# Merged jobs, a turn for each pair of scores, and a new order of work in a fused transformer layer

## The reference

```python
h = token_table[x] + segm_table[mask] + pos            # (8, 1024, 192)
n = layernorm(h)                                       # 192 channels
q, k, v = split(n @ w_qkv.T)                           # 12 heads of 16
q = layer_norm(q) * 16 ** -0.5; k = layer_norm(k)      # over the 16 of a head
h = h + (softmax(q @ k.T) @ v) @ w_proj.T              # 1024 x 1024 scores a head
xq = round(clip(layernorm(h) / mean(alpha_a1), -8, 7)) # 4-bit values
x1 = clip(gelu((xq @ wq1.T) * alpha_w1 * mean(alpha_a1) + b1), -10, 10)   # 768 wide
hq = round(clip(x1 / mean(alpha_a2), -8, 7))
out = h + (hq @ wq2.T) * alpha_w2 * mean(alpha_a2) + b2
```

## Time and profile before

| | us |
|---|---|
| median of 3 runs (1069.35 to 1070.07) | 1069.4 |
| profiled execution, span from its first to its last instruction | 1067.6 |
| PE busy (92%) | 979.4 |
| ACT busy (82%) | 872.6 |
| DVE busy (76%) | 813.9 |
| POOL busy (39%) | 411.8 |

### The profile page before, as it was taken

One profiled execution on the slowest core, in us unless ns is written; L12 is line 12 of the kernel. 1 busy time (PEld: TensorE's weight loads), 2 busy tenths in 40 slices (PEclk: granted clock), 3 DMA queues, 4 the chain that ended last, 5 costly groups with the idle time before them and its releaser, 6 DMA issues.

```text
span 1067.6 us, 19577 instructions
## 1 busy us (share of the span) xinstructions
PE 979.4 (92%) x7571; PEld 389.1 (36%) x7571; DVE 813.9 (76%) x2325; ACT 872.6 (82%) x950; POOL 411.8 (39%) x345
## 2 busy tenths in 40 slices
PE   5589999999999999999999999999999999989885
PEld 4333433334342433434343343434334343413223
DVE  5878869788686969878696977869697886825347
ACT  1387788897979889797988979798888989798883
POOL 6555513635343353534435363443526412201000
PEclk9899999999999999999999999999999999999997
DMA  7511200303011040202102040110202000000000
GB/s 162 127 16 16 31 1 2 46 1 64 12 25 22 1 75 1 38 8 58 18 2 45 1 73 3 31 16 16 30 1 45 1 16 1 16 1 1 16 1 31
DMA packets 25762, 28.62 MB, mean 27 GB/s; under 512 B 5027, under 2 KB 22182, under 8 KB 25670
## 3 DMA queue, kind: packets, MB, share of 16 engines
q0 software_dynamic: 16896, 11.80, 9.4%
q1 hardware_dynamic: 8624, 15.55, 4.8%
q10 hardware_dynamic: 150, 0.01, 0.0%
HBM read 21.06 MB, written 6.29 MB: 26 GB/s over the span
## 4 chain that ended last, share of the span: by engine, by line
PE 40%; ACT 30%; DVE 24%; issue 3%; POOL 3%; DMA 0%
ACT probs L682 22%; PE ps_o L1247 12%; PE ps_s L1227 8%; PE ps_j L1271 4%; ACT gelu L676 4%; PE ps_j L1279 3%; PE ps_j L1325 3%; POOL stack L592 3%; PE ps_j L1286 2%; PE ps_j L1292 2%; ACT L676 2%; ACT L682 2%; DVE hn L797 2%; PE ps_j L1311 2%; PE ps_j L1296 2%
## 5 line engine op out<-in xcount | busy, mean ns | idle before, releaser
L682 ACT ACTIVATE probs<-ps_s 128x1024 f32<-128x1024 f32 x768 | 736.1, 1023 | 125.5 <-PE ps_s L1227 120.6
L1247 PE MATMUL ps_o<-probs,v_sb 128*32 128x512 f32 x3072 | 394.7, 605 | 0.2 <-DVE o_sb L859 0.2
L1227 PE MATMUL ps_s<-qT,kT 64*128 64x512 f16 x1536 | 264.3, 384 | 35.0 <-ACT probs L682 25.2
L592 POOL TENSOR_TENSOR stack<-sq,stack 128x384 f16<-128x384 f32 x124 | 120.5, 992 | 162.9 <-DVE stack L846 162.9
L1227 PEld LDWEIGHTS ps_s<-qT,kT 64*128 64x128 f16 x1536 | 61.5, 93 | 299.5 <-ACT probs L682 267.6
L525 POOL DMA_INDIRECT h_all<-in_L_tok_token_table,idx x60 | 96.7, 1611 | 59.5 <-DMA h_all<-in_L_tok_segm_table,idx 41.2
L1247 PEld LDWEIGHTS ps_o<-probs,v_sb 128*32 128x32 f32 x3072 | 69.1, 109 | 124.3 <-issue 116.1
L601 POOL TENSOR_TENSOR y_sb<-y_sb,b_row 128x768 f32<-128x768 f32 x14 | 25.4, 1814 | 198.8 <-DVE y_sb L931 198.8
L581 POOL TENSOR_TENSOR sq<-qk 128x384 f32<-128x384 f32 x56 | 46.2, 826 | 139.5 <-DVE qk L894 139.5
L525 POOL DMA_INDIRECT h_all<-in_L_tok_segm_table,idx x56 | 87.2, 1557 | 15.2 <-issue 13.1
L1279 PE MATMUL ps_j<-wh,partsT 128*128 128x384 f16 (+1 forms) x384 | 71.5, 296 | 1.0 <-ACT partsT L663 0.7
(11 more groups left out here) (201 smaller groups left out, 1118.5 us busy)
## 6 DMA issues: line engine op xcount, KB each, us to landing
out<-h_all SPq DMA_DIRECT2D x15, 384.0 KB
h_all<-in_positions SPq DMA_DIRECT2D x7, 768.0 KB
gelu<-in_L_ffn_w SPq DMA_DIRECT2D x2, 576.0 KB
h_all<-in_L_tok_token_table,idx POOLq DMA_INDIRECT x60
h_all<-in_L_tok_segm_table,idx POOLq DMA_INDIRECT x56
probs<-in_L_attn_qkv_weight SPq DMA_DIRECT2D x2, 432.0 KB, 4.7
h_all<-in_positions SPq DMA_DIRECT2D x2, 384.0 KB, 8.0
o_nat<-in_L_ffn_alpha_a SPq DMA_DIRECT2D x1, 384.0 KB
```

Of the source, the lines that this page charges most:

```text
L592: last = nc.gpsimd.tensor_tensor(low, src, high, ALU.subtract)
L682: nc.scalar.activation(probs[:, u % PROBS, 2 * pair:2 * pair + 2], ps_s[:, 2 * pair:2 * pair + 2], ACT.Exp, scale=SCORE_SCALE).then_inc(ex ...
L1227: last = mm(ps_s[:, j], kT[rows, par, head // 2, m * P:(m + 1) * P], qT[rows, par, head // 2, nh * NQ:(nh + 1) * NQ], start=True, stop=True)
L1247: last = mm(ps_o[32 * j:32 * j + 2 * D, :], v_sb[:, par, m, (GH * group + j) * VE:(GH * group + j) * VE + 2 * D], probs[:, u % PROBS, j], ...
```

## The change

1. **Turns.** The plan has a new word s: one pair of scores on PE, one exp on ACT, in the place where it stands. The 48 words of a half-step are spread among heads and jobs; in START_PLAN each line simply begins with s s. The gelus stand at their word g.
2. **Merged jobs**, from half-step 1 on: A, C, G, H and Y take two tiles, I four. Their matmuls write side by side in one bank, and there is one eviction for them. Both norms (N and m) are cut in two, for two tiles each.
3. **A new order** of all words. GpSimd's work has words too: q (square), L (low halves), p (segment gather), t (token gather), a (add the result). W takes banks by its number, as X and B do.
4. n waits for the transposes of D as well as of E before it writes the high halves.

The waits count merged jobs by a function `count`; the rest of the diff replaces `nth` by it.

```diff
 
 
 PLAN = """
-h h o
-Y0 Y1 Y2 F0 Y3 F1
-G0 F2 F3 H0 G1 P0
-h h
-G2 G3 W0 W1 W2 H1 H2 H3
-h l0 h R0
-W3 m0 h
-W4 h
-h N0 W5 I0
-I1 h o A0
-I2 h A1 A2
-h A3 I3
-C0 B0 X0
-X1 B1 r0 X2 X3 B2 X4 X5 r1 B3 h r2 h r3 g h
-h
-h S0 n0
-h n1 o
-D0 x0 E0 C1
-n2 h C2 D1
-E1 n3 h
-D2 h x1
-h D3 E2 x2
-E3 x3 x4 h
-x5 C3 h
+s h o h s
+s F0 q0 F1 F2 s
+s F3 q1 G0 h s
+s G1 P0 H0 s
+s H1 s h W0
+s s h h W1
+s s q2 q3 l0 R0 Y0 W2
+s N0 h s W3
+s h m0 s A0 W4
+s h s h m1 N1 W5
+s s B0 I0
+s s A1 Y1 B1 X0 o p0 X1 r0 B2 r1 X2 x0 X3 g B3 r2 X4 r3 X5 h h
+s S0 L0 n0 s h h
+s s x1 h
+s L1 C0 n1 s o
+s h s h L2
+s s n2 h
+s E0 x2 D0 s h
+s s C1 D1
+s h s h
+s s L3 n3 E1 E2 D2 x3
+s h s
+s h s E3 D3
+s h x4 t0 x5 a0 s
 """
 
 
@@ START_PLAN @@
-h
-h n1.1 D0.1 E0.1 n2.1
...
-w1.2 h D3.2 E3.2
+s s h
+s s h n1.1 D0.1 E0.1 n2.1
...
+s s w1.2 h D3.2 E3.2 q0.2 q1.2 q2.2 q3.2 L0.2 L1.2 L2.2 L3.2
@@ banks @@
-IN_TURN = [w for w in JOBS if w[0] not in "XB"]
+TILES = {"A": 2, "C": 2, "G": 2, "H": 2, "Y": 2, "I": 4}
+IN_TURN = [w for w in JOBS if w[0] not in "XBW"]
+def tiles_of(kind, s0):
+    return TILES.get(kind, 1) if s0 >= 1 else 1
@@ GpSimd, one half-step @@
-                add_result(s0, s)
                 ahead = s0 + GATHER_AHEAD
-                if FIRST_GATHERED <= ahead < HALVES:
-                    add_segments(ahead)
-                    add_tokens(ahead)
-                square(s0, s)
-                split_low(s0, s)
+                for kind, t, at in step_work(s0):
+                    if kind == "a":
+                        add_result(s0, s)
+                    elif kind == "p" and FIRST_GATHERED <= ahead < HALVES:
+                        add_segments(ahead)
+                    elif kind == "t" and FIRST_GATHERED <= ahead < HALVES:
+                        add_tokens(ahead)
+                    elif kind == "q":
+                        square(s0, s, t)
+                    elif kind == "L":
+                        split_low(s0, s, t)
@@ ACT, one half-step @@
-                for u in range(UNITS):
...
+                for kind, t, at in step_work(s0):
+                    if kind == "g" and job_runs("X", s0):
                         for j in range(HB):
                             gelu_out(s0, s, j)
...
+                    elif kind == "s" and attends(s0):
+                        exps(s0, s, t // 2, t % 2)
@@ DVE first_norm (second_norm alike) @@
-                for t in range(TH):
+                here = slice(0, TH) if s0 <= 0 else slice(2 * i, 2 * i + 2)
+                for t in range(TH)[here]:
@@ DVE split_qk @@
+                    dve.wait_ge(job_mm["D"], half * TH + (t - 1))
                     dve.wait_ge(job_mm["E"], half * TH + (t - 1))
@@ DVE, eviction of H and Y @@
-                    tt(h_tile(half, t), ps[:, 0:C], h_tile(half, t), ALU.add).then_inc(job_out["H"], 1)
+                    two = h_all[:, at:at + 2 * C]
+                    tt(two, ps[:, 0:2 * C], two, ALU.add).then_inc(job_out["H"], 1)
...
-                    tt(y_sb[:, t], ps[:, 0:C], s2_row[:], ALU.mult).then_inc(job_out["Y"], 1)
+                    tt(y_sb[:, first:first + 2], ps[:, 0:2 * C].rearrange("p (t c) -> p t c", c=C),
+                       s2_row[:].unsqueeze(1).broadcast_to([P, 2, C]), ALU.mult).then_inc(job_out["Y"], 1)
@@ PE scores @@
-                for j in range(GH):
-                    if j % 2 == 0 and (u or attends(s0 - 1)):
-
-                        pe.wait_ge(exp_done, 2 * UNITS * s + (2 * u - 1 + j // 2))
+                if u or attends(s0 - 1):
+
+                    pe.wait_ge(exp_done, 2 * UNITS * s + (2 * u - 1 + pair))
+                for j in (2 * pair, 2 * pair + 1):
@@ PE job G (A, H, I, Y alike) @@
-                    for k in range(2):
-                        last = nc.tensor.transpose(ps[0:KC, k * P:(k + 1) * P], o_nat[:, t, k * KC:(k + 1) * KC], ident[:])
+                    for n, tile in enumerate(tiles):
+                        for k in range(2):
+                            last = nc.tensor.transpose(ps[0:KC, (2 * n + k) * P:(2 * n + k + 1) * P],
+                                                       o_nat[:, tile, k * KC:(k + 1) * KC], ident[:])
@@ PE, one half-step @@
-                for u in range(UNITS):
-                    if attends(s0):
-                        scores(s0, s, u)
-                    for kind, t, at in unit_work(s0)[u]:
...
+                for kind, t, at in step_work(s0):
+                    if kind == "s" and attends(s0):
+                        scores(s0, s, t // 2, t % 2)
```

More of the change, by code:

```diff
@@ L211, in bank_of, with count @@
         return START_JOBS.index((job, s0)) % BANKS
-    return {"X": t % 2, "B": 2}[kind] if kind in "XB" else IN_TURN.index(job) % BANKS
+    return {"X": t % 2, "B": 2, "W": t % BANKS}[kind] if kind in "XBW" else IN_TURN.index(job) % BANKS
+def tiles_of(kind, s0):
+    return TILES.get(kind, 1) if s0 >= 1 else 1
+def count(kind, half, t):
+    per, tiles = PER_HALF[kind], TILES.get(kind, 1)
+    whole = min(half, FIRST_MERGED.get(kind, 0))
+    merged = max(min(half, LAST_MERGED.get(kind, HALVES)) - whole, 0)
+    rest = half - whole - merged
+    own = tiles if whole == FIRST_MERGED.get(kind, 0) and half < LAST_MERGED.get(kind, HALVES) else 1
+    return (whole + rest) * per + merged * (per // tiles) + t // own + 1
 def jobs_of(s0):
@@ L656, in copy_out @@
                 half = job_half(kind, s)
-                act.wait_ge(job_mm[kind], nth(half, t, TH))
+                act.wait_ge(job_mm[kind], count(kind, half, t))
                 if kind == "B":
@@ L885, in job_result @@
                 half, h0 = job_half(kind, s), job_half(kind, s0)
-                job = (kind, t)
+                job, first = (kind, t), t * tiles_of(kind, s0)
                 ps = bank(job, s0)
@@ L890, in job_result @@
                         continue
-                    dve.wait_ge(job_mm[kind], nth(half, t, TH))
+                    dve.wait_ge(job_mm[kind], count(kind, half, first))
                     if kind in "BC":
@@ L1236, in heads @@
                 if u == 0 and s0 % 2 == 0:
-                    pe.wait_ge(job_out["C"], (s + (2 if s0 else 1)) * TH)
+                    pe.wait_ge(job_out["C"], count("C", s + 1 if s0 else 0, TH - 1))
                 if s0 == 0 and u == UNITS // 2:
@@ L1277, in job @@
                     passes = [(m, high[:, m]) for m in range(KP)] + [(m, low[:, m]) for m in range(KP - 1)]
-                    for n, (m, w) in enumerate(passes):
-                        last = mm(ps[:, 0:hi - lo], partsT[:, t, m], w, start=(n == 0), stop=(n == len(passes) - 1))
+                    for i, tile in enumerate(tiles):
+                        for n, (m, w) in enumerate(passes):
+                            last = mm(ps[:, i * C:i * C + hi - lo], partsT[:, tile, m], w,
+                                      start=(n == 0), stop=(n == len(passes) - 1))
                 if kind in "DE":
@@ L1393, in tail @@
                 for t in range(TH):
[L1394 removed]
+                    pe.wait_ge(job_out["F"], count("F", LAST, t))
                     result_last(LAST - 1, t, ps_s[:, t, 0:C])
```

277 lines of the change are left out of this document (146 added, 131 removed).

## The result

The changed kernel takes 1039.2 us (median of four runs, 1038.7 to 1040.1) beside 1069.7 for the kernel before on the same chip (four runs, 1069.35 to 1070.16): ratio 0.971, 95% interval 0.970 to 0.973. The forecast was 1040. The profiled execution spans 1036.9 us, 30.7 less than that of before.

A forecast was written before the change was run, and what follows sets the result against it. No engine alone bounds it: PE needs 57.0 us and ACT 53.5 of each 61.6 us half-step, the rest lost to waits. Gains of 27 (steps 1 to 13) and 2.6 (14 and 15), taken as 29.5, give 1040 us; range 1030 to 1060.

The forecast's parts named there:

- the walk: Timing of one new half-step line by line from PE's start-to-start prices: 59.2 us, where it was 61.6.
- F0's wait: At the join of half-steps, F0 waits for the copy of the last heads: 0.8 us, 0.3 reaching the end.
- The added 0.3 for small waits: Allowance per half-step for small eviction waits that a walk by durations misses, making the period 59.5 us.
- the 75 I gave as the sign: ACT's idle time before exps was to fall from 120.6 to some 75 us.
- the full 2.1: Gain in us claimed for each of half-steps 1 to 13, together 27 us.
- The price of a change-over: On PE, switching from scores to something else costs 0.10 us: a lone pair 0.32, a double 0.54.
- rival C: Separate turns of scores cost what they save, as switches drain TensorE: period 61.5, 1069 us; chance 0.04.
- 0.04 us a job: PE's saving for each of 13 jobs merged away per half-step, together 0.6 us.
- The cover I named: PE's queue hides VectorE's chain: late inputs N0 for A0, E3 and A1 come 1.2 to 1.4 us early.
- The gelu block (D): Slower: PE must leave the block within 9.8 us, without slack; 3.0 us late gives 1081 us; chance 0.06.
- The token gather (E): Slower: gather, 1.8 us early, arrives late for the next half-step's statistics; 6 us late gives 1080 us; chance 0.04.
- A: Waits come back elsewhere, halving the gain to 1 us of 2.1 per half-step: 1054 us; chance 0.18.

The follow-up runs named there:

- experiment 3: Experiment 1 with each second pair of scores given its own turn behind the first heads or job of its line: 1118.9 us, ratio 1.046.
- experiment 4: Experiment 2 with only a job, never heads, put between the two pairs of scores, in twelve units: 1084.5 us, ratio 1.014.
- experiment 5: Old order with doubled scores in the new code, but jobs A, C, G, H, Y, I merged: 1118.6 us, ratio 1.046.
- experiment 7: Changed kernel with every merged job split into single jobs side by side, new order and turns kept: 1119.1 us, ratio 1.046.
- experiment 11: Changed kernel with the last VectorE operation of each x done twice: 1113.3 us, ratio 1.039.
- experiment 12: Changed kernel with GpSimd's addition of the result put ahead of the token gather: 1071.8 us, ratio 1.002.
- experiment 9: Changed kernel with W2, W3 and W5 moved earlier in half-step 1: 1042.1 us, ratio 0.974.
- experiment 10: Changed kernel with the edits of experiments 8 and 9 together: 1038.6 us, ratio 0.972.
- experiment 8: Changed kernel with GpSimd's addition of the result waiting until x5 is quantised: 1039.4 us, ratio 0.973.
- experiment 1: New code with the old plan: single jobs, doubled scores, old GpSimd order, norms still cut in two: 1083.5 us, ratio 1.014.
- experiment 2: Experiment 1 with both norms whole again: 1075.6 us, ratio 1.005.
- experiment 6: Changed kernel with the separate turns undone, both pairs of scores at each line's head, order and merges kept: 1101.8 us, ratio 1.029.

## Why the prediction was right, and which of its steps were not

**The bound and the walk held.** PE 57.3, ACT 53.5 and a walk of 58.9 (59.2 with F0's wait) against 58.83 measured. The added 0.3 for small waits wasn't needed, and F0's wait was 0.37 where I had 0.8. ACT's idle pieces behind F0 (0.64, 0.47, 0.30, 0.46, then 0.29 at a time) lie where the walk put them and are smaller, but there are more of them behind the gelus than it had (0.31, 0.29, 0.45, 0.29, 0.30, 0.29, 0.57). Its total before exps is 86.7, not the 75 I gave as the sign. Eleven periods thus gave 30.1 us where 2.1 each would be 23.1.

**Where the surplus went.** I gave half-step 1 the full 2.1; it lost 2.4, an error of 4.5. The walk was made for a half-step without W, and W's six words with their evictions were never walked. Half-step 13 gave 0.75 instead of 2.1, because what is last there is GpSimd's addition, which a missing gather had moved onto x3. Half-step 14 came out at 57.16 (57.0). Half-step 15 and the tail gave 0.4 where I had 1.3, the start 0.6 where I had nothing. So 1040 beside 1039.2 holds two errors that cancel: 7.0 too little in the middle, 5.9 too much in half-steps 1 and 13. That the forecast is within 1 us is luck; that a full half-step gains some 2.7 us, by waits, is not.

**Turns.** The price of a change-over was right: 0.32, and rival C fell by its sign. Right too was that the gain is mostly in PE's waits: 1.8 of the 2.8 us in a half-step are idle time, and part of the other 1.0 is hidden waits. What the prediction lacked is the condition: in the old order turns lose 35 and 9 us (experiments 3 and 4), 21 and 9 of them as busy time of PE, for change-overs, that no saved wait pays for.

**Merged jobs.** 0.04 us a job was the wrong kind of price. It is the cost of an instruction, while a merge changes who gets which bank and how much stands between a job and its eviction. Experiments 5 and 7, 35 and 80 us the wrong way, are such effects in places that I gave the jobs. The rests in both (0.3 us less work of PE in a half-step, 0.9 at the most) lie around the 0.5 that thirteen times 0.04 makes, and don't prove it.

**VectorE.** I had it relieved by 2 us of evictions and up to 3 of contention per half-step. Its busy time rose by 15.7 us in all. The contention moved from the n operations with two SBUF inputs to x:
```profile
634.39 3.03 DVE L917 TENSOR_SCALAR hq<-gelu 128x512 bf16<-128x512 f32 x1
...
634.76 2.37 POOL L623 TENSOR_TENSOR stack<-sq,stack 128x384 f16<-128x384 f32 x2
```
One such operation of 0.43 takes 3.03, as long as GpSimd's two beside it and a little more (637.42 against 637.13). The group's mean was 427 ns before and is 833. That it cost nothing in time was right for the place it has, and only there: experiment 11 puts the last such operation some 1.4 us later, experiment 12 the addition some 6.7 us earlier (1.8 us behind the start of the last low halves, not 8.5), and they lose 74 and 33 us. The cover I named (1.2 to 1.4 us) was real, and thin. The Trainium skill, SBUF — State Buffer, Who interferes with whom, counts `tensor_scalar` among the operations that can take the port pair which VectorE shares with GpSimd, and has the loser wait for the whole instruction of the other. By that rule x is as much at risk as the n operations that I looked at, and the trace agrees in so far as the operation ends only behind GpSimd's, in 634.39 above and in 702.30 of experiment 11. The same section says that whoever issues first gets the pair. This the trace doesn't bear out: by the profile VectorE's operation starts 0.37 and 0.41 us ahead of GpSimd's and is the one that waits, though starts on GpSimd are rough.

**The gelu block (D)** left 9.26 us after its start where I had 9.8 at most, and ACT has no idle time behind the table load. **The token gather (E)**: its last issue ends at 656.25 and the statistics start at 661.41 with no wait for a DMA. Experiment 12 shows that 3.3 us between the two are enough, so here 1.9 and more are left. The issues beside VectorE's x operations took 1.53 and 1.54 us, so the starved descriptors of the rule that I weighed there are not seen in their durations. **A**, waits that come back elsewhere, is what half-steps 1 and 13 are, at two places instead of at all.

**Open.** Whether single jobs with an order of their own would reach 1039; what decides that the clock falls behind one wait and not behind another of the same length; why the start is 2 us longer in experiments 9 and 10; and whether the edits of experiments 8 and 10 gain anything, since their medians (1039.4, 1038.6) lie within the scatter of their runs (1037 to 1044). No version here has a median more than 0.6 us below that of the changed kernel.

## What to carry to other kernels

In queues that run in order, price the parts of a change together and by a walk of the whole period: every version short of the whole (experiments 1 to 7) was slower here than the kernel before, by 6 to 50 us, and the whole gained 30. A turn cut out of a double costs its change-over in every version (a lone pair takes 0.32, one in a double 0.27), and pays only where a wait goes with it. Walk every stage that has work of its own (the first with W, the last without a gather) and not only the steady one. And where a GpSimd tensor operation can meet a VectorE one, write down by how many microseconds they miss each other, since an edit that uses this up costs a multiple of its own work.

## What the hardware showed that I had not expected

- A VectorE operation with one SBUF input, `tensor_scalar` from f32 to bf16, 128x512, takes 0.43 us alone and 3.03 and 3.11 beside GpSimd tensor operations; its f32 neighbour 0.49 alone and 1.93. Beside an issue of the token gather alone it takes 0.43 (652.90, the issue from 652.87 on). A copy from PSUM across the start of GpSimd's L1 (638.99, 0.69) took what it takes alone.
- A wait of PE can cost twice. After 4.02 us of waiting the granted clock was 0.70 for 5.8 us, after 2.20 us 0.66 over a stretch of 5 us, after 2.63 us 0.72 over 6.2 us; after 2.64 us in another run it stayed at 1.00. In experiment 6 a wait of 2.2 us comes at the same place of ten half-steps, and behind seven of them the clock fell. The kernels with long waits have the lower mean clock, 0.963 in experiments 7 and 11 against 0.985 in the changed kernel.
